# Step one's nucleus search: Newton and secant steps on GpSimd instead of halvings, and no verifying pass on VectorE

## The chip, the cores and the metric

The kernel runs on one core of a Trainium2 chip. The metric is the device time of one execution, in microseconds. The core's engines run side by side and meet only through semaphores: TensorE (PE, with its weight loads as PEld), VectorE (DVE), ScalarE (ACT), GpSimd (POOL) and SyncE (SP), which here issues all DMAs.

## The reference, cut to what matters

```python
h = relu(layernorm(x)); x = x + A @ (h @ W + b) / deg        # x is 3327 x 256, adj 3327 x 3327
X = relu(layernorm(x))
for s in range(2):                                            # STEPS
    A = adj_from_feats(Xa, W1, W2, W3)
    Xf, Xb, Xa = Rf @ Xf, Rb @ Xb, A @ Xa
    Z = Z + Xf @ U1[s] + Xb @ U2[s] + Xa @ U3[s]
# out = x + layernorm(X + Z) * gamma + beta

def adj_from_feats(Xa, W1, W2, W3):
    logits = (Xa @ W1) @ W2 @ (Xa @ W3).T
    # each row: sort, softmax, keep the largest entries until their sum reaches P_NUC = 0.9,
    # the rest to -inf, softmax again
```

So for each of the 3327 rows a cut has to be found in 3327 exponentials: the smallest set of the largest entries that holds 0.9 of the row's sum. The kernel doesn't sort; it searches a threshold.

## The kernel before, in words

Rows go in T = 26 tiles of 128. Three blocks follow one another: the transposed adjacency and the first layer; a short middle block; and `diffusion_step(s)` for s = 0 and 1 ("step zero" and "step one"), which is where the change lies. In a step the engines run the same sweep over i from -2 to 27, each its own instruction stream in the written order; in one body, i is the tile whose sums with the adjacency run on PE (L1398), j = i+1 the tile in the second half of its search, m = i+2 the tile whose logits come in, k = i-1 the tile whose masked exponentials are multiplied with xa. The exponentials of a tile live in one of three buffers `pb`.

In step one the path of a tile is: PE makes its logits in four chunks (L1317). VectorE takes them out of PSUM (`take_logits`, L1206) and reduces the negated row maximum (`negmax`, L1211). ScalarE exponentiates with a row sum (L878). Then the search: in each of 3 + 3 levels ScalarE makes two sums at the present threshold t, the sum of relu and the sum of sign (L896 and L901, `sums`). The first three levels (SUB = ROUGH[1] = 3) look at 832 of the columns (WSUB), the other three at all 3327. GpSimd turns the sums of a level into the mass above t, compares it with the target and moves t up or down by a fixed factor (`level`, L797 to L825); it then lets ScalarE go on (L823) or, after the last level, VectorE (L825). Most instructions there are linked: each waits for the one before.

VectorE (`search`, from L1009) waits for `p_ready`, picks the tightest bracket from the points tried (`bracket`), interpolates a threshold in it (`towards`), makes a verifying pass over all columns at it (L1061), puts the result into the bracket (L1063 to L1066), interpolates again, and makes the cut pass (L1070), which keeps what lies below the cut. It takes the eight largest of each of 16 segments (L1075), then the first chunks of logits of tile m; sorts the candidates in five rounds of eight (L1080, L1082), taking the other logits after the second round; a prefix sum (L1093) finds the exact boundary; 16 MATCH_REPLACE8 take the kept values out (L1134), and the mask pass L1137 subtracts the rest from `pb`. PE then transposes (L1344), ScalarE copies to `pt` (L920), PE multiplies with `xa` (L1352). If the boundary does not lie among the sorted values, `settle` (L1227 on) does more rounds over the whole tile.

What sets the order: ScalarE's body is pt 0, pt 1, z copy, sums of j's level three, pt 2, pt 3, sums of j's level four, xo, exponential of m, sums of m's level zero, the two sums of j's level five with the copies to zt between, sums of m's level one, t_hi and t256, sums of m's level two, t_hi and t256 again. GpSimd's body is `spread` of k (L781), `add_z` (L787), the identity added to `at` (L838), levels three and four of j, the goal and level zero of m, level five of j, levels one and two of m. Tile 0 of step one has only the three subset levels on ScalarE; VectorE makes its three full ones as passes (L1023).

Of the kernel before, what the change touches and what calls it, by code (L numbers as in the profile page):

```python
# [44 lines left out]
def gnn_program(nc, x, adj, W, b, W1, W2, W3, U1, U2, U3, gamma, beta, out):  # L45
# [29 lines left out]
    AIM = (6.0, 16.0)  # L75
    CUT_AIM = (6.0, 24.0)
    VERIFIED = (0, 1)
# [3 lines left out]
    MARGIN = 0.45  # L81
    MOVES = []
    for rough, fine in zip(ROUGH, BISECTIONS):
        half = RANGE / 2 ** (rough + 1) + (MARGIN if rough else 0.0)
        MOVES.append([RANGE / 2 ** (e + 2) for e in range(rough)] + [half / 2 ** (e + 1) for e in range(fine)])
    GMAX, RMAX = max(SEGMENTS), max(SORTED)
    KMAX = 2 + max(b + v for b, v in zip(BISECTIONS, VERIFIED)) + 1
# [3 lines left out]
    FIRST_BISECTIONS = (1, 0)  # L91
# [23 lines left out]
    def sb(name, shape, dt):  # L115
        return nc.alloc_sbuf_tensor(name, shape, dt)
# [35 lines left out]
    padone = sb("padone", [P, 1], f32)  # L152
    early = below[:, :]
# [54 lines left out]
    lower, upper = ends[:, 0:4:2], ends[:, 1:4:2]  # L208
    cur = sb("cur", [P, 2], f32)
    is_lower = sb("is_lower", [P, 1], i32)  # L210
    is_upper = sb("is_upper", [P, 1], i32)
# [13 lines left out]
    over = [sb(f"over{u}", [P, 8], f32) for u in range(3)]  # L225
# [105 lines left out]
    with nc.Block() as block:  # L331
# [39 lines left out]
        def _(pool):  # L371
            nc.gpsimd.memset(ident[:, :], 0.0).then_inc(sem("const_chain"), 1)
            nc.gpsimd.memset(padone[:, :], 1.0).then_inc(sem("const_chain"), 1)
            for u in range(2):
                nc.gpsimd.memset(adj_in[u][:, N:NP], 0.0).then_inc(sem("adj_pad"), 1)
# [297 lines left out]
    def diffusion_step(s):  # L673
# [4 lines left out]
        def S(name):  # L678
            return sem(f"step_{name}")
# [23 lines left out]
        with nc.Block() as block:  # L703
# [67 lines left out]
            def _(pool):  # L771
# [17 lines left out]
                def goal(j):  # L789

                    u = j.third
                    pool.wait_ge(S("exp"), j.n + 1)
                    share = nucleus_pad[:, :] if j.t == T - 1 else NUCLEUS
                    nc.gpsimd.tensor_scalar(targets[u][:, :], mass[u][:, 0:1], share, None, ALU.mult)
                    ch.link(nc.gpsimd.tensor_scalar(over[u][:, 5:6], mass[u][:, 0:1], (NUCLEUS - 1.0) * WSUB / N, None, ALU.mult))

                def level(j, e):  # L797
# [4 lines left out]
                    if e == 0:  # L802
                        goal(j)
                    o, g = over[u], f + 1
                    t = rough_t[u][:, e:e + 1] if f < 0 else thr[u][:, 2 + f:3 + f]
                    up, down = math.exp(MOVES[s][e]), math.exp(-MOVES[s][e])
                    pool.wait_ge(S3("sums")[u], levels_before(s, j.t) + e + 1)
                    ch.link(nc.gpsimd.tensor_scalar(o[:, 2:3], o[:, 1:2], float(WSUB if f < 0 else N), t, ALU.add, ALU.mult))  # L808
                    if f < 0:
                        m, enough = o[:, 3:4], o[:, 5:6]  # L810
                        ch.link(nc.gpsimd.tensor_scalar(m, o[:, 2:3], -0.5, o[:, 0:1], ALU.mult, ALU.add))  # L811
                    else:
                        m, enough = mass[u][:, 2 + f:3 + f], targets[u][:, :]
                        ch.link(nc.gpsimd.tensor_scalar(m, o[:, 2:3], 0.5, o[:, 0:1], ALU.mult, ALU.add))
                    if g < BISECTIONS[s]:
                        ch.link(nc.gpsimd.tensor_scalar(o[:, 4:5], m, enough, up - down, ALU.is_ge, ALU.mult))  # L816
                        if g < 0:
                            ch.link(nc.gpsimd.tensor_scalar(rough_t[u][:, e + 1:e + 2], o[:, 4:5], down, t, ALU.add, ALU.mult))  # L818
                        else:
                            ch.link(nc.gpsimd.tensor_scalar(thr[u][:, 2 + g:3 + g], o[:, 4:5], down, t, ALU.add, ALU.mult))  # L820
                            if not last:
                                ch.link(nc.gpsimd.tensor_scalar(minus_t[u][:, g:g + 1], thr[u][:, 2 + g:3 + g], -1.0, None, ALU.mult))
# [4 lines left out]
                pool.wait_ge(S("search_consts"), 1)  # L827
                ch = Chain(pool, f"step_levels_{s}")
# [37 lines left out]
            def _(act):  # L866
# [13 lines left out]
                def sums(j, n):  # L880
# [6 lines left out]
                    t, sign = (rough_t[u][:, e:e + 1], -1.0) if e < SUB else (minus_t[u][:, e - SUB:e - SUB + 1], 1.0)  # L887
                    before = levels_before(s, j.t)
# [103 lines left out]
            def _(dve):  # L992
# [16 lines left out]
                def search(i):  # L1009
# [8 lines left out]
                    for e in range(AB, BISECTIONS[s]):  # L1018
# [6 lines left out]
                        if e < BISECTIONS[s] - 1:  # L1025
                            d = MOVES[s][SUB + e]
# [413 lines left out]
```

## Time and profile before

| | us |
|---|---|
| median of 3 runs | 2397.59 (2395.61 to 2397.72) |
| the profiled execution, its span | 2397.4 (no other time of it is given) |
| PE busy | 1968.8 (82%) |
| VectorE busy | 1946.8 (81%) |
| ScalarE busy | 1708.7 (71%) |
| GpSimd busy | 873.0 (36%) |
| mean granted TensorE clock | 0.932 |

Rows of the trace give a start and a length in us, the engine, the line, the operation, out<-in, and in brackets how long the engine was idle before and who ended the idle time. "POOLq" or "DVEq" is an engine's sequencer, which issues the semaphore increments that stand alone. Times of instructions are from one profiled execution.

### The profile page before, as it was taken

The page shows a single profiled execution, that of the slowest core. Times are in us where ns is not written, and L with a number is a line of the kernel's source. Part 1 is how long each engine was busy: PE and PEld are TensorE (multiplying, and loading weights), DVE is VectorE, ACT ScalarE, POOL GpSimd, SP SyncE. Part 2 cuts the span into 40 slices and gives each one's busy share as a digit, 9 for nine tenths or more (in the row PEclk, how much of TensorE's full clock was granted, in tenths as well). Part 3 has the DMA queues.
Part 4 walks back from the last instruction along what each step waited for, and adds up shares of the span by engine and source line. Part 5 has one row for each costly group of instructions (what it writes and reads, how often), then busy time and mean ns, then how long its engine had stood idle before and what let it go on. Part 6 is the DMA issues. An engine that isn't in the chain of part 4 may idle for free. (4 is left out here: it accounts for less than half of the span.)

```text
span 2397.4 us, 33017 instructions
## 1 busy us (share of the span) xinstructions
PE 1968.8 (82%) x10002; PEld 1296.6 (54%) x10002; DVE 1946.8 (81%) x6082; ACT 1708.7 (71%) x1806; POOL 873.0 (36%) x1438
## 2 busy tenths in 40 slices
PE   2999753999999999999945979798888888888883
PEld 1555322666666666666623555565655556555552
DVE  6777657788888888888647888988888888898885
ACT  4443236888888888888437888888887888888840
POOL 2000042344444444444433353443435344343423
PEclk9999876999999999999977999999898999999996
DMA  6777221011111111111160001001010100101023
GB/s 229 280 282 289 95 97 36 28 50 50 50 50 48 50 50 46 39 43 50 41 228 18 21 21 40 21 21 41 21 40 21 41 21 21 41 21 40 20 70 125
DMA packets 65726, 167.62 MB, mean 70 GB/s; under 512 B 7037, under 2 KB 45307, under 8 KB 61947
## 3 DMA queue, kind: packets, MB, share of 16 engines
q1 hardware_dynamic: 65530, 165.43, 19.9%
q8 instruction: 72, 1.18, 0.2%
q14 instruction: 124, 1.02, 0.1%
HBM read 117.95 MB, written 47.45 MB: 69 GB/s over the span
## 5 line engine op out<-in xcount | busy, mean ns | idle before, releaser
L1352 PE MATMUL banks<-xa,pt 128*128 128x256 f32 x2704 | 683.3, 407 | 126.0 <-ACT pt L920 125.9
L1352 PEld LDWEIGHTS banks<-xa,pt 128*128 128x128 f32 x2704 | 533.4, 203 | 283.3 <-ACT pt L920 139.6
L896 ACT ACTIVATE junk_a<-pb_all,minus_t 128x3327 f16<-128x3327 f32 x151 | 463.9, 3072 | 150.1 <-POOLq L823 147.5
L901 ACT ACTIVATE junk_a<-pb_all,minus_t 128x3327 f16<-128x3327 f32 x151 | 463.3, 3068 | 2.6
L1398 PE MATMUL banks<-region,at 128*128 128x512 f16 x2028 | 450.4, 381 | 0.0
L808 POOL TENSOR_SCALAR over<-over,points 128x1 f32<-128x1 f32 x151 | 164.7, 1091 | 740.5 <-ACT junk_a L901 740.4
L1398 PEld LDWEIGHTS banks<-region,at 128*128 128x128 f16 x2028 | 199.5, 98 | 231.1 <-issue 6.0
L1206 DVE TENSOR_SCALAR_CACHE_REDUCE pb_all<-banks 128x1024 f32<-128x1024 f32 x260 | 210.9, 849 | 96.6 <-PE banks L1317 93.8
L1317 PE MATMUL banks<-keys,qs 64*128 64x512 f32 (+1 forms) x832 | 199.8, 576 | 90.8 <-DVE pb_all L1206 50.2
L1344 PE MATMUL banks<-ident,pb_all 128*128 128x128 f32 x1352 | 191.7, 291 | 54.5 <-DVE pb_all L1137 34.4
L1075 DVE MAX8 junk_v<-below 128x8 f32<-128x208 f32 (+1 forms) x624 | 222.5, 432 | 2.2
L878 ACT ACTIVATE pb_all<-pb_all,negmax 128x3327 f32<-128x3327 f32 x52 | 159.4, 3065 | 72.4 <-DVE negmax L1211 72.4
L920 ACT ACTIVATE pt<-banks 128x896 f32<-128x896 f32 x208 | 173.0, 861 | 51.1 <-PE banks L1344 50.2
L1344 PEld LDWEIGHTS banks<-ident,pb_all 128*128 128x128 f32 x1352 | 168.6, 151 | 68.6 <-issue 56.8
L1070 DVE SCALAR_TENSOR_TENSOR below<-pb_all,cur 128x3327 f32<-128x3327 f32 x52 | 203.8, 3920 | 1.9
L1317 PEld LDWEIGHTS banks<-keys,qs 64*128 64x128 f32 x832 | 69.8, 193 | 176.6 <-DVE pb_all L1206 71.0
L1023 DVE SCALAR_TENSOR_TENSOR below<-pb_all,points 128x3327 f32<-128x3327 f32 x31 | 114.2, 3685 | 51.9 <-POOLq L825 51.8
L533 PE MATMUL banks<-region,at 128*128 128x512 f16 x676 | 151.5, 381 | 0.0
L1406 PE MATMUL banks<-u_sb,zt 128*128 128x256 f32 x624 | 148.5, 388 | 1.1 <-ACT zt L956 1.1
L1134 DVE MATCH_REPLACE8 below<-junk_v,below 128x208 f32<-128x208 f32 x416 | 143.6, 359 | 0.0
L896 ACT ACTIVATE junk_a<-pb_all,rough_t 128x832 f16<-128x832 f32 x78 | 77.1, 989 | 75.1 <-POOLq L823 72.0
L1406 PEld LDWEIGHTS banks<-u_sb,zt 128*128 128x128 f32 x624 | 114.3, 190 | 16.7 <-ACT zt L953 1.5
(222 smaller groups left out, 2914.1 us busy)
## 6 DMA issues: line engine op xcount, KB each, us to landing
at<-adjT_d SPq DMA_DIRECT2D x52, 832.0 KB, 4.9
region<-in_adj_dram SPq DMA_DIRECT2D x25, 1663.5 KB, 7.9
adjT_d<-at SPq DMA_DIRECT2D x26, 832.0 KB, 3.9
fb_d<-fb_sb SPq DMA_DIRECT2D x26, 256.0 KB, 2.0
region<-fb_d SPq DMA_DIRECT2D x2, 3328.0 KB, 18.1
y_d<-y_sb SPq DMA_DIRECT2D x50, 128.0 KB, 1.9
x_d<-pb_all SPq DMA_DIRECT2D x1, 3328.0 KB, 10.4
qs<-q_d SPq DMA_DIRECT2D x104, 32.0 KB, 4.2
```

The costliest lines, as they stand in the source:

```text
L808: ch.link(nc.gpsimd.tensor_scalar(o[:, 2:3], o[:, 1:2], float(WSUB if f < 0 else N), t, ALU.add, ALU.mult))
L896: nc.scalar.activation(junk_a[:, 0:w], pb[u][:, 0:w], ACT.Relu, scale=sign, bias=t, accum_out=over[u][:, 0:1])\
L901: nc.scalar.activation(junk_a[:, 0:w], pb[u][:, 0:w], ACT.Sign, scale=sign, bias=t, accum_out=over[u][:, 1:2])\
L920: nc.scalar.activation(pt[sl][:, 0:n * P], pt_ps[sl][:, 0:n * P], ACT.Copy).then_inc(S2("pt")[sl], 1)
L1070: ch.link(nc.vector.scalar_tensor_tensor(out=below[:, 0:N], in0=p, scalar=cut, in1=p, op0=ALU.is_lt, op1=ALU.mult, accum_out=below_sum[:, :]))
L1075: ch.add(nc.vector.max(cand[:, 8 * g:8 * g + 8], below[:, g * W8:(g + 1) * W8]))
L1206: nc.vector.tensor_scalar(halves_of_p[:, h:h + n, a:a + w], halves_of_bank[:, h:h + n, 0:w], 1.0, -3.0e38, ALU.mult, ALU.max, accum_out=mi ...
L1317: nc.tensor.matmul(pt_ps[c % 2][:, h * CW:h * CW + w], qs[j.slot][r, :], keys[r, s * HW + c0:s * HW + c0 + w], start=True, stop=True).then ...
L1344: last = nc.tensor.transpose(pt_ps[sl][:, t * P:(t + 1) * P], p[:, (t0 + t) * P:(t0 + t + 1) * P], ident[:, :])
L1352: last = nc.tensor.matmul(bank[4][:, 0:D], pt[sl][:, t * P:(t + 1) * P], xa[:, t0 + t, :], start=(t0 + t == 0), stop=(t0 + t == T - 1))
L1398: last = nc.tensor.matmul(bank[5 + n][:, :], at[i.slot][:, t, :], mov, start=(t == 0), stop=(t == T - 1))
L1406: last = nc.tensor.matmul(bank[7][:, 0:D], zt[:, q, :], u_sb[:, q // KD, q % KD, :], start=(q == 0), stop=(q == 5))
```

## The change

In step one a level no longer moves the threshold by a fixed factor. From the two sums GpSimd gets the count and the sum of the entries below t. On the three subset levels it makes a Newton step for the sum below to equal the wanted tenth; on the first full level a Newton step that aims beyond the target by OVERSHOOT thresholds to one side or the other; on the second full level a secant step from the last two points, with an aim of 12; the third full level only notes its mass. Each step has a division, made as a power of -1 (`ALU.pow` with `minus_one`, a new constant). ScalarE reads the threshold with a sign of -1, so the negated copy `minus_t` goes in step one. The goal has an instruction more. VectorE's verifying pass, its comparisons and its second interpolation go; the cut's aim is 20 instead of 24 thresholds. Tile 0 of step one has a fourth level on ScalarE and GpSimd, and VectorE makes its other two full levels as passes, with a secant step between them. Step zero keeps its halvings; its goal has one instruction less.

```diff
-    AIM = (6.0, 16.0)
-    CUT_AIM = (6.0, 24.0)
-    VERIFIED = (0, 1)
+    CUT_AIM = (6.0, 20.0)
+    OVERSHOOT = 20.0
+    SECANT_AIM = 12.0
...
-    FIRST_BISECTIONS = (1, 0)
+    FIRST_BISECTIONS = (1, 1)
...
+                    ch.link(nc.gpsimd.tensor_scalar(targets[u][:, :], mass[u][:, 0:1], share, None, ALU.mult))
+                    ch.link(nc.gpsimd.tensor_tensor(over[u][:, 8:9], mass[u][:, 0:1], targets[u][:, :], ALU.subtract))
+                    ch.link(nc.gpsimd.tensor_scalar(over[u][:, 5:6], over[u][:, 8:9], WSUB / N, None, ALU.mult))
+
+                def newton(j, e):
...
+                    ch.link(nc.gpsimd.tensor_scalar(count, o[:, 1:2], float(WSUB if f < 0 else N), 0.5, ALU.add, ALU.mult))
+                    ch.link(nc.gpsimd.tensor_scalar(low, count, t, gap, ALU.mult, ALU.subtract))
+                    if f >= 0:
+                        ch.link(nc.gpsimd.tensor_scalar(mass[u][:, 2 + f:3 + f], low, -1.0, mass[u][:, 0:1], ALU.mult, ALU.add))
+                    if f < 1:
+                        ch.add(nc.gpsimd.tensor_scalar(count, count, low, 1e-20, ALU.mult, ALU.max))
+                        if f < 0:
+                            ch.link(nc.gpsimd.tensor_scalar(b, low, wanted, gap, ALU.subtract, ALU.mult))
+                        else:
+                            ch.add(nc.gpsimd.tensor_scalar(a, low, wanted, 2.0 * OVERSHOOT, ALU.is_ge, ALU.mult))
+                            ch.link(nc.gpsimd.tensor_scalar(b, low, wanted, 2.0, ALU.subtract, ALU.mult))
+                            ch.link(nc.gpsimd.tensor_scalar(a, a, OVERSHOOT, t, ALU.subtract, ALU.mult))
+                            ch.link(nc.gpsimd.tensor_scalar(b, b, a, gap, ALU.add, ALU.mult))
+                        ch.link(nc.gpsimd.tensor_tensor(count, count, minus_one[:, :], ALU.pow))
+                        ch.link(nc.gpsimd.tensor_scalar(b, b, count, t, ALU.mult, ALU.subtract))
+                        if f < 0:
+                            ch.link(nc.gpsimd.tensor_scalar(to, b, -1.0, 0.5, ALU.mult, ALU.min))
+                        else:
+                            ch.link(nc.gpsimd.tensor_scalar(b, b, -1.0, 1.0, ALU.mult, ALU.min))
+                            ch.link(nc.gpsimd.tensor_scalar(to, b, 1e-5, None, ALU.max))
+                    elif f == 1:
+                        ch.add(nc.gpsimd.tensor_scalar(b, t, SECANT_AIM, low, ALU.mult, ALU.subtract))
+                        ch.add(nc.gpsimd.tensor_tensor(a, t, thr[u][:, 2:3], ALU.subtract))
+                        ch.link(nc.gpsimd.tensor_tensor(low, low, o[:, 6:7], ALU.subtract))
+                        ch.add(nc.gpsimd.tensor_scalar(count, low, low, 1e-16, ALU.mult, ALU.max))
+                        ch.link(nc.gpsimd.tensor_scalar(b, b, wanted, a, ALU.add, ALU.mult))
+                        ch.link(nc.gpsimd.tensor_tensor(count, count, minus_one[:, :], ALU.pow))
+                        ch.link(nc.gpsimd.tensor_scalar(b, b, low, count, ALU.mult, ALU.mult))
+                        ch.link(nc.gpsimd.tensor_scalar(b, b, t, 1.0, ALU.add, ALU.min))
+                        ch.link(nc.gpsimd.tensor_scalar(to, b, 1e-5, None, ALU.max))
...
+                    if not first and e >= SUB:
+                        t, sign = thr[u][:, 2 + e - SUB:3 + e - SUB], -1.0
...
-                    for v in range(VERIFIED[s]):
-                        towards(cur[:, 0:1], AIM[s])
-                        ch.link(nc.vector.scalar_tensor_tensor(out=below[:, 0:N], in0=p, scalar=cur[:, 0:1], in1=p,
-                                                               op0=ALU.is_ge, op1=ALU.mult, accum_out=cur[:, 1:2]))
-                        nc.vector.tensor_scalar(is_lower[:, :], cur[:, 1:2], tg, None, ALU.is_ge)
-                        ch.link(nc.vector.tensor_scalar(is_upper[:, :], cur[:, 1:2], tg, None, ALU.is_lt), hold=True)
-                        nc.vector.copy_predicated(lower, is_lower[:, :].to_broadcast([P, 2]), cur[:, :])
-                        ch.link(nc.vector.copy_predicated(upper, is_upper[:, :].to_broadcast([P, 2]), cur[:, :]))
                     towards(cur[:, 0:1], CUT_AIM[s])
```

On a subset level f is below 0; f = 0, 1, 2 are the three full levels. In `newton`, as before, two increments follow the instructions: `point`, for which ScalarE's next sums wait, and after the last level `p_ready`, for which VectorE waits.

## Rows read from the trace of the kernel before

**Rows 1.** Busy time by engine in a stretch, step one's steady part; columns as headed.

```profile
core 0: us, PE busy (x) PEld busy (x) DVE busy (x) ACT busy (x) POOL busy (x), PEclk, DMA share, GB/s
1323.48:2249.11 925.63, 794.55 (x3742) 524.33 (x3740) 811.75 (x3080) 759.69 (x837) 386.54 (x682) 0.93 0.09 28
```

**Rows 2.** Chain of waits through step one: start us, us, what.

```profile
1323.48 2.95 issue
...
1659.32 2.95 issue
...
1680.75 6.24 PE banks L1352 x14
...
1702.15 2.95 issue
...
1723.58 4.98 PE banks L1352 x14
...
1743.89 2.95 issue
...
2249.11 2.95 issue
```

**Rows 3.** VectorE's waits, 1323.48 to 2249.11: us in total, times, longest us.

```profile
DVE pb_all L1206 <- PE banks L1317: 67.0, 44, 3.0
```

**Rows 4.** Timeline of three engines in one turn: start us, us, engine, line.

```profile
1755.61 3.62 DVE L1137 TENSOR_TENSOR pb_all<-pb_all,below 128x3327 f32<-128x3327 f32 x1
...
1756.41 2.95 POOL L808 TENSOR_SCALAR over<-over,points 128x1 f32<-128x1 f32 x1 [5.53 <-ACT junk_a L901]
...
1759.46 0.27 POOL L814 TENSOR_SCALAR points<-over 128x1 f32<-128x1 f32 x1
...
1760.01 0.29 POOL L808 TENSOR_SCALAR over<-over,rough_t 128x1 f32<-128x1 f32 x1 [0.29 <-POOL points L814]
...
1760.40 0.27 POOL L811 TENSOR_SCALAR over<-over 128x1 f32<-128x1 f32 x1
...
1760.77 0.29 POOL L816 TENSOR_SCALAR over<-over 128x1 f32<-128x1 f32 x1
...
1761.15 0.31 POOL L818 TENSOR_SCALAR rough_t<-over,rough_t 128x1 f32<-128x1 f32 x1
...
1761.55 0.99 ACT L896 ACTIVATE junk_a<-pb_all,rough_t 128x832 f16<-128x832 f32 x1 [2.22 <-POOLq L823]
...
1762.11 3.68 DVE L1061 SCALAR_TENSOR_TENSOR below<-pb_all,cur 128x3327 f32<-128x3327 f32 x1
...
1763.84 2.09 POOL L808 TENSOR_SCALAR over<-over,rough_t 128x1 f32<-128x1 f32 x1 [2.38 <-ACT junk_a L901]
```

**Rows 5.** GpSimd's groups by line, whole run: busy us, mean ns, idle before.

```profile
L822 POOL TENSOR_SCALAR minus_t<-points 128x1 f32<-128x1 f32 x125 | 27.9, 223 | 10.9
...
L620 POOL TENSOR_SCALAR region<-xa 128x256 f16<-128x256 f32 x26 | 25.4, 978 | 27.1 <-ACT xa L638 25.1
```

**Rows 6.** Timeline where step one begins, around 1294 to 1303.

```profile
1294.30 3.69 DVE L1061 SCALAR_TENSOR_TENSOR below<-pb_all,cur 128x3327 f32<-128x3327 f32 x1
1294.32 3.74 POOL L816 TENSOR_SCALAR over<-over 128x1 f32<-128x1 f32 x1
...
1298.50 0.99 ACT L896 ACTIVATE junk_a<-pb_all,rough_t 128x832 f16<-128x832 f32 x1 [4.30 <-POOLq L823]
...
1302.28 1.22 PE L1352 MATMUL banks<-xa,pt 128*128 128x256 f32 x2 [10.10 <-ACT pt L920]
```

**Rows 7.** Busy time and granted clock in the first product's beginning, columns as rows 1.

```profile
1680.70:1683.90 3.20, 3.15 (x8) 2.52 (x9) 2.95 (x15) 2.10 (x3) 2.57 (x7) 0.50 0.00 0
```

**Rows 8.** ScalarE's timeline in the head of step one.

```profile
1237.01 0.99 ACT L901 ACTIVATE junk_a<-pb_all,rough_t 128x832 f16<-128x832 f32 x1
...
1264.86 3.07 ACT L896 ACTIVATE junk_a<-pb_all,minus_t 128x3327 f16<-128x3327 f32 x1 [3.59 <-POOLq L823]
```

**Rows 9.** Timeline near the end of step one, tile 25's full levels.

```profile
2287.66 0.44 PE L1385 MATMUL banks<-ident,xo_sb 128*128 128x128 f32 x2 [1.92 <-ACT xo_sb L938]
...
2289.70 3.07 ACT L896 ACTIVATE junk_a<-pb_all,minus_t 128x3327 f16<-128x3327 f32 x1 [2.10 <-POOLq L823]
```

More of the change, by code:

```diff
@@ L80, in gnn_program @@
     WSUB = (N + 1) // 4
[L81 to L85, printed above, removed]
+    MOVES = [RANGE / 2 ** (e + 2) for e in range(BISECTIONS[0])]
     GMAX, RMAX = max(SEGMENTS), max(SORTED)
-    KMAX = 2 + max(b + v for b, v in zip(BISECTIONS, VERIFIED)) + 1
+    KMAX = 2 + max(BISECTIONS) + 1
     MOST = max(ACT_BISECTIONS)
-    FIRST_BISECTIONS = (1, 0)
+    FIRST_BISECTIONS = (1, 1)
     LEVELS = [[r + f] + [r + a] * (T - 1) for r, f, a in zip(ROUGH, FIRST_BISECTIONS, ACT_BISECTIONS)]
@@ L152, in gnn_program @@
     padone = sb("padone", [P, 1], f32)
+    minus_one = sb("minus_one", [P, 1], f32)
     early = below[:, :]
@@ L207, in gnn_program @@
     lows, highs = ends[:, 1:3], ends[:, 0:4:3]
[L208 to L211, printed above, removed]
+    cur = sb("cur", [P, 1], f32)
     frac = sb("frac", [P, 4], f32)
@@ L224, in gnn_program @@
     minus_t = [sb(f"minus_t{u}", [P, MOST], f32) for u in range(3)]
-    over = [sb(f"over{u}", [P, 8], f32) for u in range(3)]
+    over = [sb(f"over{u}", [P, 12], f32) for u in range(3)]
     unsettled = sb("unsettled", [P, 1], f32)
@@ L793, in goal @@
                     share = nucleus_pad[:, :] if j.t == T - 1 else NUCLEUS
-                    nc.gpsimd.tensor_scalar(targets[u][:, :], mass[u][:, 0:1], share, None, ALU.mult)
-                    ch.link(nc.gpsimd.tensor_scalar(over[u][:, 5:6], mass[u][:, 0:1], (NUCLEUS - 1.0) * WSUB / N, None, ALU.mult))
+                    if first:
+                        nc.gpsimd.tensor_scalar(targets[u][:, :], mass[u][:, 0:1], share, None, ALU.mult)
+                        return
+                    ch.link(nc.gpsimd.tensor_scalar(targets[u][:, :], mass[u][:, 0:1], share, None, ALU.mult))
@@ new lines, in goal @@
+                    ch.link(nc.gpsimd.tensor_tensor(over[u][:, 8:9], mass[u][:, 0:1], targets[u][:, :], ALU.subtract))
+                    ch.link(nc.gpsimd.tensor_scalar(over[u][:, 5:6], over[u][:, 8:9], WSUB / N, None, ALU.mult))
+                def newton(j, e):
+                    u, last, f = j.third, e == LEVELS[s][j.t] - 1, e - SUB
+                    o = over[u]
+                    t = rough_t[u][:, e:e + 1] if f < 0 else thr[u][:, 2 + f:3 + f]
+                    to = rough_t[u][:, e + 1:e + 2] if f < -1 else thr[u][:, 3 + f:4 + f]
+                    count, gap = o[:, 2:3], o[:, 0:1]
+                    low = o[:, 6 + f:7 + f] if f in (0, 1) else o[:, 3:4]
+                    wanted = o[:, 5:6] if f < 0 else o[:, 8:9]
+                    a, b = o[:, 9:10], o[:, 10:11]
+                    ch.link(nc.gpsimd.tensor_scalar(count, o[:, 1:2], float(WSUB if f < 0 else N), 0.5, ALU.add, ALU.mult))
[28 more added lines that the diff above has]
+                        ch.link(nc.gpsimd.tensor_scalar(to, b, 1e-5, None, ALU.max))
+                    pool.sem_inc(S3("point")[u], 1)
+                    if last:
+                        pool.sem_inc(S("p_ready"), 1)
@@ L803, in level @@
                         goal(j)
+                    pool.wait_ge(S3("sums")[u], levels_before(s, j.t) + e + 1)
+                    if not first:
+                        newton(j, e)
+                        return
                     o, g = over[u], f + 1
-                    t = rough_t[u][:, e:e + 1] if f < 0 else thr[u][:, 2 + f:3 + f]
-                    up, down = math.exp(MOVES[s][e]), math.exp(-MOVES[s][e])
-                    pool.wait_ge(S3("sums")[u], levels_before(s, j.t) + e + 1)
@@ L808, in level @@
[L808 to L814, printed above, removed]
+                    t = thr[u][:, 2 + f:3 + f]
@@ L815, in level @@
+                    up, down = math.exp(MOVES[e]), math.exp(-MOVES[e])
+                    ch.link(nc.gpsimd.tensor_scalar(o[:, 2:3], o[:, 1:2], float(N), t, ALU.add, ALU.mult))
+                    m, enough = mass[u][:, 2 + f:3 + f], targets[u][:, :]
+                    ch.link(nc.gpsimd.tensor_scalar(m, o[:, 2:3], 0.5, o[:, 0:1], ALU.mult, ALU.add))
                     if g < BISECTIONS[s]:
                         ch.link(nc.gpsimd.tensor_scalar(o[:, 4:5], m, enough, up - down, ALU.is_ge, ALU.mult))
[L817 to L822, printed above, removed]
+                        ch.link(nc.gpsimd.tensor_scalar(thr[u][:, 2 + g:3 + g], o[:, 4:5], down, t, ALU.add, ALU.mult))
+                        if not last:
+                            ch.link(nc.gpsimd.tensor_scalar(minus_t[u][:, g:g + 1], thr[u][:, 2 + g:3 + g], -1.0, None, ALU.mult))
```

18 lines of the change are left out of this document (16 added, 2 removed).

## The prediction

> **What bounds the kernel now.** I read, in this order, the busy shares of step one's steady stretch, the chain of waits through it, who waits for whom, and one tile's timeline. In the stretch no engine is full: of 925.6 us PE is busy 794.6, VectorE 811.8, ScalarE 759.7, GpSimd 386.5 [rows 1]. So it is a loop of latencies, and the reader should look for what repeats. The chain [rows 2] repeats once a tile at each exponential: 42.83 us for one tile, 41.74 for the next; from 1323.48 to 2249.11 there are 22 turns, 42.07 on average. A turn, seen from the exponential at 1743.89, is: exponential and two short sums on ScalarE; two full sums; GpSimd's last level of tile j (L808, L814); GpSimd's level one of tile m; ScalarE's two subset sums, the t_hi copies and the first pt copy; then PE's products and logits; VectorE's last take of logits; next exponential. VectorE is on this loop after the logits only: from there to the mask pass (L1137) the diff changes nothing. Before the logits it waits for PE, 67.0 us in 44 waits, about 3 a tile [rows 3]. The verifying pass lies there, in VectorE's slack.
>
> What VectorE does to GpSimd matters more. L808, ready at 1756.41, takes 2.95 us and ends when the mask pass, 1755.61 + 3.62, does; L808 at 1763.84 takes 2.09 and ends just behind the verifying pass, 1762.11 + 3.68. Undisturbed neighbours take 0.27 to 0.31 [rows 4]. A VectorE pass over two SBUF operands holds back any GpSimd instruction that follows it, to its end. By SBUF — State Buffer in the Trainium skill, section "Who interferes with whom", a DVE instruction with two SBUF inputs contends with a GpSimd instruction that reads SBUF, and the second fully blocks; the trace agrees (2.95 and 2.09 against 0.3). Were the port shared by bandwidth instead, the same change would give the second rival below.
>
> **What goes.** Per tile: the pass of 3.68 [rows 4] and about a dozen small VectorE instructions, some 5.5 us. VectorE then waits for PE that much longer: gain on the loop 0, since the last logits and all behind them come when PE brings them. The cut pass (L1070) moves up into the very place of the verifying pass, as soon as the bracket and one `towards` are done, so the port is not free there either; only the second meeting, with `spread`, goes, and that is off the loop. minus_t goes on two levels, ScalarE's sums cost the same.
>
> **What comes, on GpSimd.** A linked instruction steps to the next in 0.37 (two constants, L811), 0.38 (one pointer, L816) or 0.41 (L808); an unlinked one costs about its duration, 0.29 [rows 4]. A subset level becomes 7 instructions, one unlinked, for 4. Their starts, from the level's first: 0, 0.37, 0.78, 1.07, 1.48 (the power), 1.78 + X, 2.19 + X (the one that writes the threshold). X is what the power costs beyond an ordinary small instruction of 0.2. No row shows a power; the bounds are the smallest instruction, 0.22, and the longest elementwise one, 128x256, 0.98 [rows 5], so X is 0 to 0.75. I take 0.3, nearer the small end as the width is one column. Levels three and four grow from 5 to 12 instructions, about 1.8 to 4.4 + X; the last from 2 to 3, +0.4; the goal from 2 to 3.
>
> **The step that decides.** Today level one of tile m starts at 1760.01 and lets ScalarE go at 1761.55; VectorE's pass starts at 1762.11: it misses the pass by 0.6 [rows 4]. Both start from the last level of tile j and shift by the same 0.41. Then the level's first instruction starts at 1760.42, its last one at 1762.61 + X, and the pass at 1762.52, or 0.03 to 0.3 later if the instruction before holds the port. The last instruction therefore falls behind the pass for every X above -0.09, and ScalarE goes on at about 1766.45 + X, 1766.75, not 1761.55: +5.2. The trace already has this case once: at 1294.30 the pass starts, at 1294.32 L816 is caught for 3.74, ScalarE idles 4.30, and PE idles 10.10 [rows 6].
>
> Next, the PE: its first product (L1352 x14) takes 4.98 in one turn and 6.24 in another [rows 2]. Where the turn has the 6.24, it lasts 42.83 instead of 41.74. After a longer idle I expect the 6.24 each time: in its first 3.2 us the granted clock was 0.50, the 1.2 GHz level, after an idle of some 4 us [rows 7], and the product behind the idle of 10.10 took about as long. So a turn is 42.83 + 5.2 = 48.0, or +6.0 on the average of 42.07.
>
> What hides the rest. Level two of tile m now starts behind the pass: unblocked it takes 2.46 + X and frees ScalarE's next full sum some 4.4 late, under the 5.2. Level three comes in front of the third full sum, and adds 2.6 + X to ScalarE's side; ScalarE is through at 45.6 of the turn, PE and VectorE bring the next maximum at 48.0: hidden, with 2 us of cover; a power of X = 2 would use it up. Level four (4.2 + X) lies beside the exponential and two short sums, 5.5 us: hidden. Level zero and the goal lie beside a full sum of 3.07: hidden. The subset levels' unblocked `spread` and `add_z` are far from any reader.
>
> **Head and tail of the step.** Tile 0 has a fourth level on ScalarE and two VectorE passes less. Today the third subset sum of tile 0 ends at 1238 and tile 1's first full sum starts at 1264.86 [rows 8]. After: two levels in front +2.7, level two 2.8, two full sums 6.4 (2 x 3.07 and readout), so about 1250; level three, 4.7; then VectorE's three passes with gaps of 1.6 and 2.3, from 1255 to 1270. Tile 1's three subset levels meet these passes and its full sum starts about 1278: +13. Its next full level adds 2.9 in front of the exponential of tile 2. Mask pass and last level no longer meet there, but level one's block is as long as today's. Head: +17. At the end tiles 24 and 25 have no exponential in front; the last subset threshold comes 4.4 late, then PE waits for xo and ScalarE for level four ([rows 9]: 1.92 and 2.10 today). Level three adds 2.9, and the last tile's VectorE chain, 5.5 shorter, gives back up to where PE's flags hold it, some 3.7: together -0.8.
>
> **Sum.** The profiled execution's span is 2397.4 (no other time of it is shown), 0.2 under the median of 2397.59. 2397.4 + 17 (head) + 22 x 6.0 = 132 + 4.4 - 0.8 = 2550.0; with the 0.2, 2550. Step zero: only its goal loses one instruction, in front of a wait: 0.
>
> **Rivals.**
> 1. *Costly power.* X = 2 rather than 0.3 (a row of 0.98 for 128x256 speaks against it, the missing row for it). ScalarE then ends later than PE: a turn of about 51.3, 22 x 9.2 = 203, head 25: 2630. At X = 0.75, still as forecast, about 2565; at X = 0, 2542.
> 2. *The level slips in front of the pass*, or the port is shared. Then only instructions count: a turn is +1.4 (0.41 and three more instructions, 1.0), and level two is caught in place of it, off PE's path: 22 x 1.4 = 31, head 15: 2443. For it: the miss is 0.09 + X only. Against: X must be negative, and a sharing port would not show 2.95 and 3.74.
> 3. *Not slower.* VectorE's relief reaches the loop through the port: level two is no longer held 1.78 a tile (2.09 less 0.31), ScalarE's full sum starts earlier and sets pt for PE. At most 22 x 1.78 = 39: 2358. This decides only if the level's three added instructions and the third of the last level together cost less than the 0.56 us by which level one now misses the pass; four instructions at 0.29 at least are 1.16 [rows 4]. Two places of the loop would have to be wrong.
> 4. *The search ends worse*: without the checked bracket a row's boundary may fall outside the 40 sorted values, and extra rounds run (L1227 on, never entered in the trace). Three full passes at 3.7 and four rounds of a maximum and a replacement over 3335 columns are some 40 us a tile. For it: 128 rows of 26 tiles must all hit. Against: three threshold points by secant lie close, and the cut aims 20 elements deep in 40. One to three tiles: 2590 to 2670.
>
> **Chances and range.** Forecast 0.73, costly power 0.09, slipping 0.10, worse search 0.04, not slower 0.04. The forecast's own range is 2530 to 2580. The range to hold 8 in 10 reaches into both neighbours, 2480 to 2620. Of the 0.04, half is faster by over 0.2%: 0.02; within 0.2%, about what a measurement of this kernel can tell from no change, 0.02; slower 0.96.
>
> **What would show it.** Turn of the chain near 48; GpSimd's last instruction of level one 3 to 4 us long and behind L1070; ScalarE's wait in front of L896 on the subset from 2.22 to about 7; PE's idle before L1352 near 9 to 10 a tile; first product near 6.2 each time; VectorE's wait before the first logits up by 5. Wrong if no threshold instruction of level one is over 0.5 us (then 2), if the power's own spacing is above 1 (then 1), if the turn stays under 42 (then 3), or if L1228 appears (then 4).

## The result, and the profile after

| | before | after |
|---|---|---|
| median of the runs taken together | 2397.65 us (2395.61 to 2399.72) | 2548.39 us (2547.39 to 2550.83) |
| profiled execution, span | 2397.4 us | 2545.9 us |
| ratio | | 1.0627, 95% interval 1.0612 to 1.0642 |

The forecast was 2550, its range 2480 to 2620. The page of the kernel after begins with busy time by engine (us, share of the span, instructions):

```profile
PE 1968.0 (77%) x10002; PEld 1292.3 (51%) x10002; DVE 1787.6 (70%) x5721; ACT 1713.1 (67%) x1810; POOL 1045.4 (41%) x2035
```

The steady part of step one, from tile 3's exponential to tile 25's, columns as in [rows 1]:

```profile
core 0: us, PE busy (x) PEld busy (x) DVE busy (x) ACT busy (x) POOL busy (x), PEclk, DMA share, GB/s
1339.97:2391.18 1051.21, 793.15 (x3742) 521.36 (x3741) 677.11 (x2772) 757.97 (x837) 543.08 (x1212) 0.89 0.08 25
```

PE and ScalarE do what they did, VectorE has 135 us less to do, GpSimd 157 more, and the stretch is 1051.21 us instead of 925.63: 22 turns of 47.78 instead of 42.07. That is 125.6 of the 148.5 us between the two spans. The head (exponential of tile 0 to that of tile 3) went from 98.4 to 116.1, +17.7; the tail from 148.3 to 154.7, +6.4; what lies before, -1.2.

One turn of the chain of waits in the kernel after (start us, us, what), for [rows 2]:

```profile
1769.77 2.95 issue
...
1782.27 2.92 POOL over L806
...
1788.49 3.89 POOL over L820
...
1792.75 1.09 ACT junk_a L938 x2
...
1796.53 5.87 PE banks L1398 x14
...
1817.55 2.95 issue
```

L806 is the first instruction of tile j's last level, held by the mask pass as L808 was before. L820 is new on the chain: it is an instruction of 0.4 us that takes 3.9. The timeline of that place shows why, for [rows 4]:

```profile
1781.51 3.62 DVE L1183 TENSOR_TENSOR pb_all<-pb_all,below 128x3327 f32<-128x3327 f32 x1
...
1782.27 2.91 POOL L806 TENSOR_SCALAR over<-over 128x1 f32<-128x1 f32 x1 [4.03 <-ACT junk_a L943]
...
1786.30 0.19 POOL L806 TENSOR_SCALAR over<-over 128x1 f32<-128x1 f32 x1 [0.28 <-POOL points L809]
...
1787.82 0.56 POOL L819 TENSOR_TENSOR over<-over,minus_one 128x1 f32<-128x1 f32 x1
...
1788.42 3.69 DVE L1116 SCALAR_TENSOR_TENSOR below<-pb_all,cur 128x3327 f32<-128x3327 f32 x1
1788.49 3.88 POOL L820 TENSOR_SCALAR over<-over,rough_t 128x1 f32<-128x1 f32 x1
...
1792.45 0.22 POOL L822 TENSOR_SCALAR rough_t<-over 128x1 f32<-128x1 f32 x1
...
1792.75 0.99 ACT L938 ACTIVATE junk_a<-pb_all,rough_t 128x832 f16<-128x832 f32 x1 [7.55 <-POOLq L836]
```

Level one of tile m begins at 1786.30. VectorE's cut pass (L1116) starts 2.12 later, 0.07 ahead of L820, which then ends 0.26 behind the end of the pass. L820 and L822, the two instructions behind the power, are thus through only after the pass, and ScalarE's subset sum, idle for 2.22 before [rows 4], is idle for 7.55. VectorE and PE wait for it in turn (who waits for whom, 1350 to 2380: us in total, times, longest):

```profile
DVE pb_all L1252 <- PE banks L1363: 309.9, 63, 11.0
...
ACT junk_a L938 <- POOLq L836: 211.0, 65, 7.9
PE banks L1398 <- ACT pt L962: 210.6, 22, 9.6
```

VectorE's wait for logits was 67.0 us [rows 3] and is 309.9, or 11.0 a turn more: the 6.1 a turn that VectorE has less to do are spent in that wait, and some 5 more. The power by itself, among GpSimd's groups by line (busy us, mean ns, idle before), beside an ordinary instruction of two inputs:

```profile
L819 POOL TENSOR_TENSOR over<-over,minus_one 128x1 f32<-128x1 f32 x104 | 58.8, 566 | 8.7
...
L828 POOL TENSOR_TENSOR over<-points 128x1 f32<-128x1 f32 x25 | 4.8, 193 | 2.0
```

### The profile page after: what moved, and what is told of

It reads as the page before. It is cut to its first block, busy times and chain, and to the rows that moved or that the text cites. A ratio compares the mean times of both kernels' runs of the same rounds, so it can differ in the third digit from the quotient of the medians.

```text
span 2545.9 us, 33233 instructions
## 1 busy us (share of the span) xinstructions
PE 1968.0 (77%) x10002; PEld 1292.3 (51%) x10002; DVE 1787.6 (70%) x5721; ACT 1713.1 (67%) x1810; POOL 1045.4 (41%) x2035
## 4 chain that ended last, share of the span: by engine, by line
PE 17%; POOL 11%; ACT 11%; issue 10%; DVE 3%; DMA 0%; POOLq 0%; ACTq 0%; DVEq 0%; SPq 0%
PE banks L1398 13%; ACT junk_a L943 5%; POOL over L820 4%; ACT junk_a L938 3%; PE banks L1363 3%; POOL over L806 3%; DVE pb_all L1252 2%; PE banks L1390 1%; POOL over L807 1%; POOL over L819 1%; ACT pt L962 1%; POOL over L813 1%; DVE region L1326 1%; DVE region L1321 0%; ACT zt L995 0%
## 5 line engine op out<-in xcount | busy, mean ns | idle before, releaser
L1398 PE MATMUL banks<-xa,pt 128*128 128x256 f32 x2704 | 694.4, 412 | 271.1 <-ACT pt L962 271.1
L1398 PEld LDWEIGHTS banks<-xa,pt 128*128 128x128 f32 x2704 | 541.8, 207 | 431.0 <-ACT pt L962 283.4
L938 ACT ACTIVATE junk_a<-pb_all,minus_t 128x3327 f16<-128x3327 f32 x76 | 233.5, 3073 | 106.4 <-POOLq L862 106.1
L806 POOL TENSOR_SCALAR over<-over 128x1 f32<-128x1 f32 x154 | 95.6, 621 | 479.9 <-ACT junk_a L943 473.3
L938 ACT ACTIVATE junk_a<-pb_all,points 128x3327 f16<-128x3327 f32 x76 | 233.4, 3071 | 69.5 <-POOLq L836 67.2
L854 POOL TENSOR_SCALAR over<-over,points 128x1 f32<-128x1 f32 x76 | 85.7, 1127 | 423.8 <-ACT junk_a L943 423.8
L943 ACT ACTIVATE junk_a<-pb_all,points 128x3327 f16<-128x3327 f32 x76 | 233.3, 3070 | 1.7
L943 ACT ACTIVATE junk_a<-pb_all,minus_t 128x3327 f16<-128x3327 f32 x76 | 233.0, 3066 | 0.9
L962 ACT ACTIVATE pt<-banks 128x896 f32<-128x896 f32 x208 | 172.9, 860 | 79.5 <-PE banks L1390 79.5
L1390 PE MATMUL banks<-ident,pb_all 128*128 128x128 f32 x1352 | 178.2, 277 | 52.8 <-DVE pb_all L1183 34.1
L1116 DVE SCALAR_TENSOR_TENSOR below<-pb_all,cur 128x3327 f32<-128x3327 f32 x52 | 192.1, 3694 | 1.9
L1390 PEld LDWEIGHTS banks<-ident,pb_all 128*128 128x128 f32 x1352 | 156.0, 143 | 66.1 <-issue 54.8
```

Of the source, the lines that this page charges most:

```text
L806: ch.link(nc.gpsimd.tensor_scalar(count, o[:, 1:2], float(WSUB if f < 0 else N), 0.5, ALU.add, ALU.mult))
L938: nc.scalar.activation(junk_a[:, 0:w], pb[u][:, 0:w], ACT.Relu, scale=sign, bias=t, accum_out=over[u][:, 0:1])\
L943: nc.scalar.activation(junk_a[:, 0:w], pb[u][:, 0:w], ACT.Sign, scale=sign, bias=t, accum_out=over[u][:, 1:2])\
L962: nc.scalar.activation(pt[sl][:, 0:n * P], pt_ps[sl][:, 0:n * P], ACT.Copy).then_inc(S2("pt")[sl], 1)
L1390: last = nc.tensor.transpose(pt_ps[sl][:, t * P:(t + 1) * P], p[:, (t0 + t) * P:(t0 + t + 1) * P], ident[:, :])
L1398: last = nc.tensor.matmul(bank[4][:, 0:D], pt[sl][:, t * P:(t + 1) * P], xa[:, t0 + t, :], start=(t0 + t == 0), stop=(t0 + t == T - 1))
```

## The experiments

The theory (the port): a long VectorE pass over two SBUF operands holds the next small GpSimd instruction to its end, so that the two engines meet not only through semaphores; the loop loses 5 us a turn because the last instructions of the longer level one no longer start before the pass does. Its rivals: the time is the sum of the instructions added; or it is the power; or it is the verifying pass's own doing.

**e1 and e2: how many small instructions until the step.** The kernel before, with idle instructions put into level one of tile m; two in e1, three in e2.

```diff
+                        for _ in range(2 if e == 1 else 0):      # e2: 3
+                            ch.link(nc.gpsimd.tensor_scalar(o[:, 7:8], o[:, 2:3], -0.5, o[:, 0:1], ALU.mult, ALU.add))
```

> The kernel before, with two more linked GpSimd instructions of one column in level one only (they write an unused column). Port theory (a VectorE pass over two SBUF operands holds the level's last instruction if that starts behind the pass): the last instruction starts at 1761.15 + 0.75 = 1761.90, still before the pass at 1762.11, so only the instructions count: a turn is +0.8, 22 turns +18, the granted clock up to 15 more: 2415 to 2435. Rival (what a level costs is the sum of its instructions, wherever the pass lies): the same, 2415.

> As the last one with three such instructions instead of two, 0.37 us more. Port theory: the last instruction would start at 1762.28, behind the pass at 1762.11, and is held to its end at 1765.8; ScalarE goes on 4.5 us later than in the kernel before, and the first product on PE takes the longer form: +5 a turn, 2500 to 2520. Rival (sum of instructions): 22 x 1.1 = 24, 2422 to 2445.

Measured: 2412.01 (ratio 1.0051, 1.0034 to 1.0067) with two, 2520.52 (1.0508, 1.0490 to 1.0525) with three; before 2399.63. Both lie outside what I had written, 3 us under the range and 0.5 over it. From e1 to e2, one instruction of 0.37 us a turn costs 108.5 us; the rival's 22 x 0.37 is 8. The turn goes from 42.64 to 47.20 on average, 4.6 more, which is 100 of it; head and tail have the rest. The first two instructions together cost 0.6 a turn. GpSimd's last instruction of the level and VectorE's verifying pass, first in e1, then in e2:

```profile
1683.93 0.26 POOL L820 TENSOR_SCALAR rough_t<-over,rough_t 128x1 f32<-128x1 f32 x1
...
1684.17 3.68 DVE L1063 SCALAR_TENSOR_TENSOR below<-pb_all,cur 128x3327 f32<-128x3327 f32 x1
```

```profile
1673.27 3.69 DVE L1063 SCALAR_TENSOR_TENSOR below<-pb_all,cur 128x3327 f32<-128x3327 f32 x1
...
1673.42 3.67 POOL L820 TENSOR_SCALAR rough_t<-over,rough_t 128x1 f32<-128x1 f32 x1
```

0.24 ahead of the pass it takes 0.26; 0.15 behind its start it takes 3.67. What counts is when the last instruction starts: in e1 it ends at 1684.19, when the pass has begun, and is not held. This is a staircase, with no Newton step, no power and no pass removed.

**e3: keep the Newton steps, and take the collision away.** The kernel after; VectorE starts the cut pass of tile i when level one of tile i + 1 has ended.

```diff
+                    if not first and (i + 1).inside(T):
+                        dve.wait_ge(S3("point")[(i + 1).third], levels_before(s, (i + 1).t) + 2)
                     ch.link(nc.vector.scalar_tensor_tensor(out=below[:, 0:N], in0=p, scalar=cut, in1=p, ...
```

> The changed kernel, and VectorE waits with the cut pass of tile i until GpSimd has finished level one of tile i+1; all work stays. Port theory: the level's two last instructions are no longer held, ScalarE goes on 3.5 us earlier in each turn, a turn of 44.2 for 47.8: 2469 (2455 to 2485), though a wait was only added. Rival (sum of instructions): no change, 2548. Rival (VectorE's own time bounds the turn): slower than 2548, as the cut pass comes later.

Measured: 2468.88 (1.0289, 1.0272 to 1.0306). In its timeline L820 is short again, and the pass pays 0.96 for it:

```profile
1669.87 0.39 POOL L820 TENSOR_SCALAR over<-over,rough_t 128x1 f32<-128x1 f32 x1
1670.35 0.22 POOL L822 TENSOR_SCALAR rough_t<-over 128x1 f32<-128x1 f32 x1
1670.72 3.68 DVE L1118 SCALAR_TENSOR_TENSOR below<-pb_all,cur 128x3327 f32<-128x3327 f32 x1 [0.96 <-POOLq L836]
```

The turn is 44.39 on average. So of the change's 5.71 a turn, 3.39 are the collision and 2.32 the instructions themselves, with whatever VectorE's wait costs. A wait added to VectorE saves 79.5 us.

**e6: the same pass, with one SBUF operand.** The kernel after; the cut pass is replaced by an instruction that reads only p. It does not cut, and the flag for further rounds is held at zero.

```diff
-  ch.link(nc.vector.scalar_tensor_tensor(out=below[:, 0:N], in0=p, scalar=cut, in1=p, op0=ALU.is_lt, op1=ALU.mult, accum_out=below_sum))
+  ch.link(nc.vector.tensor_scalar(below[:, 0:N], p, 1.0, -3.0e38, ALU.mult, ALU.max, accum_out=below_sum))
```

> The changed kernel with step one's cut pass made by an instruction that reads one SBUF operand (times 1, maximum, with accumulator) and so doesn't cut; the flag for extra rounds is held at zero. The pass is as long. Port theory: with one SBUF operand it doesn't hold GpSimd, level one's last two instructions run through, a turn of about 44.2: 2469 (2450 to 2485). Rival (any long VectorE instruction that writes SBUF slows GpSimd): no change, 2548.

Measured: 2463.75 (1.0269, 1.0252 to 1.0286), a turn of 44.39 like that of e3. L820 starts inside the pass and is not held:

```profile
1709.54 3.62 DVE L1120 TENSOR_SCALAR_CACHE_REDUCE below<-pb_all 128x3327 f32<-128x3327 f32 x1
1709.61 0.39 POOL L820 TENSOR_SCALAR over<-over,rough_t 128x1 f32<-128x1 f32 x1
```

Of the passes seen here, those with two SBUF operands hold GpSimd and this one does not. The Trainium skill says in SBUF — State Buffer, "Who interferes with whom", that a VectorE instruction with two SBUF inputs contends with a GpSimd instruction that reads SBUF, and that one with at most one SBUF input, outside the modes that use both ports, does not. This run agrees with it: same place, same width, one operand fewer, no hold (0.39 against 3.88).

**e7: the power replaced by an addition.** The kernel after; its thresholds are then not the search's, and the flag is held at zero.

```diff
-  ch.link(nc.gpsimd.tensor_tensor(count, count, minus_one[:, :], ALU.pow))
+  ch.link(nc.gpsimd.tensor_tensor(count, count, minus_one[:, :], ALU.add))
```

> The changed kernel with each power on GpSimd replaced by an addition, so the thresholds are not those of the search; the flag for extra rounds is held at zero. It measures the power's own price: 0.37 us (0.56 against 0.19). Port theory: the instruction behind the power now starts 0.3 before the pass, but the last one still behind it: a turn is shorter only by what comes behind the pass, 0.3: with the head 2538 (2530 to 2545). Rival (the powers' cost adds up, five a turn): 22 x 1.9 = 41 less, 2507.

Measured: 2533.39 (1.0559, 1.0542 to 1.0577). The instruction falls from 566 to 190 ns, the kernel by 15.0 us, the turn from 47.78 to 47.44. The held instruction is now the last one, L822, as the prediction had it for the kernel after:

```profile
1780.11 3.69 DVE L1116 SCALAR_TENSOR_TENSOR below<-pb_all,cur 128x3327 f32<-128x3327 f32 x1
1780.26 3.61 POOL L822 TENSOR_SCALAR rough_t<-over 128x1 f32<-128x1 f32 x1
```

It misses by 0.15, where the prediction's 0.09 + X gives 0.09. So X = 0 is not enough to slip ahead of the pass; where the limit lies no run shows.

**e4: the Newton steps with the verifying pass put back.**

```diff
+                    for v in range(VERIFIED[s]):        # VERIFIED = (0, 1), AIM = (6.0, 16.0)
+                        towards(cur[:, 0:1], AIM[s])
+                        ...
                     towards(cur[:, 0:1], CUT_AIM[s])
```

> The changed kernel with the verifying pass, its comparisons and second interpolation back on VectorE: so the GpSimd part of the change alone. Port theory: the verifying pass stands where the cut pass was and holds level one just as long; the cut pass now holds level two, which frees ScalarE's full sum 2.6 later and makes ScalarE the last to come: a turn of 49.1, 2577 (2560 to 2595). Rival (the work taken from VectorE counts in full): +5.5 a turn, 2670.

Measured: 2617.81 (1.0910, 1.0892 to 1.0928): a miss, 41 us above the theory's value and 23 above its range. The rival, +5.5 a turn, is out: an undisturbed turn is 48.76 (forecast 49.1), 0.98 more than the kernel after's, which gives 22 x 0.98 = 21.6; tile 3's exponential comes 7.3 later. What was not foreseen is in one tile near the end: between the exponentials at 2176.13 and 2360.35 lie three turns and 37.9 us more. The chain of waits there:

```profile
2240.34 3.63 DVE pb_all L1286
2244.00 3.70 DVE below L1287 x2
...
2248.11 3.65 DVE top L1273
...
2252.84 3.62 DVE below L1212
```

These are the further rounds of the search, entered once, for four rounds. The kernel after enters them nowhere; why the pass put back leaves one tile unsettled that was settled without it stays open. Of the 72.1 us between the spans of the two kernels (2618.0 and 2545.9) the other 5 lie behind tile 25's exponential. So in the changed kernel, unlike in the old one (e5), the verifying pass would not be free: it would cost about 1 us a turn.

**e5: the halvings without the verifying pass.** The kernel before, with the flag for further rounds held at zero.

```diff
-    VERIFIED = (0, 1)
+    VERIFIED = (0, 0)
-    ... tensor_tensor(unsettled[:, :], none[:, :], flaw[:, :], ALU.max)
+    ... tensor_tensor(unsettled[:, :], none[:, :], none[:, :], ALU.subtract)
```

> The kernel before without the verifying pass, comparisons and second interpolation, and with the flag for extra rounds held at zero in step one, so that rows whose boundary lies outside the sorted values get no extra rounds: the VectorE part of the change alone. Port theory: VectorE only waits longer for the logits and the cut pass stands in the verifying pass's place: turn 42.1 as before, head a few us shorter: 2392 (2385 to 2399). Rival (VectorE's relief counts in full): 22 x 5.5 = 121 less, 2277.

Measured: 2391.10 (0.9969, 0.9959 to 0.9979). Some 3.68 us and a dozen small instructions a tile less on VectorE bring 8.0 us in the kernel. Its turns are 41.73 and 42.75, as before's, and 42.04 on average: the gain is outside them. The forecast "gain on the loop 0" holds; the rival, full relief at 2277, is out.

**e9: the same, with the further rounds kept.** e5's first edit alone.

```diff
-    VERIFIED = (0, 1)
+    VERIFIED = (0, 0)
```

> The kernel before without the verifying pass, and with the further rounds of the search kept. If the halvings leave all rows of all 26 tiles settled without that pass, the time is that of the run in which these rounds were shut off, 2391 (2385 to 2399). If the pass is what keeps rows settled (my rival of a worse search, taken over to the old search), each tile that enters the further rounds costs about 38 us, the price that one such entry had in the run of the new search with the verifying pass put back: 2430 for one, 2470 for two, more for more.

Measured: 96461.66 us, 40.2 times the time of before (40.14 to 40.27). Neither of the two values that I had written came near. VectorE's largest groups:

```profile
L1214 DVE MAX8 top<-below 128x8 f32<-128x3335 f32 x10712 | 38937.1, 3635 | 3140.4 <-issue 3138.0
L1153 DVE MATCH_REPLACE8 below<-take,below 128x3335 f32<-128x3335 f32 x10712 | 38745.9, 3617 | 0.0
```

10712 rounds at 8.78 us each ((96461.7 - 2388.9) / 10712) are the whole difference. The kernel runs the rounds in fixed blocks of 4, 24 and 416; a block that is entered runs whole. In the trace all 26 tiles of step one enter (L1228 x26), two leave after 28 rounds, and 24 run all 444: they had a row that was still open after 28 rounds. How many rounds those rows needed can't be read from it. With these halvings and this aim of the cut (24) the verifying pass can't be left out, and e5 is a measurement of time only: in the old kernel the pass is free in time and keeps the search out of its further rounds. I forecast a price of 38 us an entry from e4, where four rounds were enough; an entry that runs all blocks costs 3.9 ms. Which rows ask for them, and why, stays open, and so does whether another aim would do without the pass.

**e8: Newton steps, with the order built for the port.** The kernel after. ScalarE makes tile m's sums of level one between tile j's last two full sums; GpSimd does level one of m ahead of level five of j; VectorE's mask pass waits for level one of i + 2, and the cut pass for level two of i + 1.

```diff
 GpSimd
+                    if not first:
+                        level(m, 1)
                     level(j, SUB + ACT_BISECTIONS[s] - 1)
 ScalarE
+                    if not first and m.inside(T):
+                        for n in range(2, 4):
+                            sums(m, n)
                     if j.inside(T):
                         for n in STEPS[NT + 1]:
                             sums(j, n)
 VectorE
+                    if not first and (i + 1).inside(T):
+                        dve.wait_ge(S3("point")[(i + 1).third], levels_before(s, (i + 1).t) + 3)
                     ... the cut pass
+                        if (i + 2).inside(T):
+                            dve.wait_ge(S3("point")[(i + 2).third], levels_before(s, (i + 2).t) + 2)
                         ch.add(nc.vector.tensor_tensor(p, p, below[:, 0:N], ALU.subtract))
```

> The changed kernel with the work ordered around the port, all work kept: ScalarE makes m's level-one sums between j's two last full sums, GpSimd does level one of m before level five of j, VectorE waits with the mask pass for level one of tile i+2 and with the cut pass for level two of tile i+1. Port theory: the wait of 2.7 behind the mask pass and that of 3.7 behind the cut pass both go from the loop; a turn of 40.5 against 47.8 and 42.1, head and tail as in the changed kernel: 2390 (2375 to 2410), the first version in which the passes taken from VectorE pay. Rival (sum of instructions): no change from 2548.

Measured: 2382.12 (0.9925, 0.9909 to 0.9942): the fastest of all, 166 us under the kernel after with the same arithmetic, and 17 under the kernel before in the same series (2399.11). The turn settles at 40.96 and is 40.85 on average. Its timeline shows GpSimd's one instruction that is still held, and VectorE's pass waiting:

```profile
1755.30 3.62 DVE L1192 TENSOR_TENSOR pb_all<-pb_all,below 128x3327 f32<-128x3327 f32 x1 [2.65 <-POOLq L836]
```

```profile
1755.00 0.22 POOL L822 TENSOR_SCALAR rough_t<-over 128x1 f32<-128x1 f32 x1
1755.61 3.36 POOL L806 TENSOR_SCALAR over<-over 128x1 f32<-128x1 f32 x1 [0.40 <-ACT junk_a L948]
```

Level one (its last instruction is L822) ends 0.08 before the mask pass starts; the held L806 belongs to level five, for which only VectorE waits.

**e11: that order without VectorE's two waits.**

> The kernel after in the new order, without the two waits of VectorE. If the hold of small GpSimd instructions by VectorE's long passes decides, the order alone gets level one into the way of the mask pass, which without its wait starts about 2.7 us earlier, ahead of the end of level one, and holds one instruction for 3.3 us or so: between 2382 and the 2548 of the kernel after, 2440 (2400 to 2480). If the length of the chain of GpSimd instructions and its place in the order decide, and not the hold, taking the waits away costs nothing: 2382 or less (2365 to 2385).

Measured: 2477.42 (1.0326, 1.0309 to 1.0344), near the upper end of the theory's range. Without the waits level one meets the mask pass, and level two the cut pass (VectorE's rows, then GpSimd's):

```profile
1706.37 3.62 DVE L1188 TENSOR_TENSOR pb_all<-pb_all,below 128x3327 f32<-128x3327 f32 x1
...
1716.06 3.68 DVE L1121 SCALAR_TENSOR_TENSOR below<-pb_all,cur 128x3327 f32<-128x3327 f32 x1
```

```profile
1706.48 3.75 POOL L807 TENSOR_SCALAR over<-over,rough_t 128x1 f32<-128x1 f32 x1
...
1716.28 3.88 POOL L819 TENSOR_TENSOR over<-over,minus_one 128x1 f32<-128x1 f32 x1
```

Each is caught within 0.22 us of the pass's start. The two waits are worth 95.3 us; the order without them is worth 71.0 against the kernel after.

**e10: the same order and waits with the halvings and the verifying pass.** The edits of e8 made to the kernel before, the first wait ahead of the verifying pass.

> The kernel before (halvings and verifying pass) in the order that made the kernel after fast: level one of tile m ahead of level five of tile j on GpSimd, its sums between the last two full sums of j on ScalarE, and VectorE's verifying and mask passes waiting for it. If what made that version fast is the order, which keeps small GpSimd instructions out of VectorE's long passes, it works as well with the shorter halvings: a turn of 40 to 41 in place of 42.07, 2355 (2335 to 2385). If the order repaired only what the Newton steps broke, nothing is gained: 2398 (2390 to 2415).

Measured: 2389.95 (0.9960, 0.9945 to 0.9974), a turn of 41.56 where I had said 40 to 41: between the two theories' ranges, at the edge of the second. The order gains 9.7 us on the kernel before of the same series (2399.64), and half a microsecond a turn. The busy time of one turn and VectorE's waits in it say what is in the way:

```profile
core 0: us, PE busy (x) PEld busy (x) DVE busy (x) ACT busy (x) POOL busy (x), PEclk, DMA share, GB/s
1653.29:1694.85 41.56, 36.50 (x171) 24.18 (x170) 37.16 (x141) 34.46 (x38) 18.07 (x31) 0.92 0.09 30
```

```profile
1666.32 3.62 DVE L1146 TENSOR_TENSOR pb_all<-pb_all,below 128x3327 f32<-128x3327 f32 x1 [1.22 <-POOLq L823]
...
1670.61 0.23 DVE L1042 TENSOR_SCALAR least<-points,target 128x5 f32<-128x5 f32 x1 [0.66 <-POOLq L825]
...
1672.81 0.16 DVE L1051 TENSOR_TENSOR frac<-ends 128x1 f32<-128x1 f32 x1 [1.08 <-POOLq L823]
```

VectorE is busy 37.16 of 41.56 and waits 2.96 for GpSimd; in this turn it waits nowhere for PE's logits. In e8's turns it still does (busy time of one, then a row of the next):

```profile
1699.86:1740.81 40.95, 36.32 (x172) 24.31 (x170) 31.25 (x127) 34.45 (x39) 25.22 (x55) 0.92 0.09 30
```

```profile
1776.38 1.23 DVE L1261 TENSOR_SCALAR_CACHE_REDUCE pb_all<-banks 128x1024 f32<-128x1024 f32 x1 [2.95 <-PE banks L1372]
```

So with level one out of the passes' way VectorE has next to no slack in e10, and the pass that goes is worth something: from e10 to e8, relief less longer levels, 7.8 us, with a turn of 40.85 for 41.56 and a head 12.5 longer. That VectorE bounds e10's turn is inferred from these sums; the chain of waits of that run does not reach back into the turns.

## Why the prediction was right, point by point

The mechanism is the one that was forecast. That 2548.39 lies within 2 us of the 2550 is partly luck: against the sum's span of 2550.0 the turns brought 6.4 less, the head 0.7 more, the tail 2.8 more and what lies before 1.2 less, which makes 2545.9, and the median of the runs lies 2.5 above that profiled span.

- **The step that decides: right.** Level one of tile m fell behind the cut pass, ScalarE went on 5 us late. I had the last instruction caught at X = 0.3; the last two were behind the pass. The cause is the size of X: the power has 566 ns, 0.37 more than the 193 of an ordinary one. So L820 started at 2.19 from the level's first instruction and not at 1.78 + 0.3 = 2.08, and the pass at 2.12 and not at 2.10: 0.07 behind it, not 0.02 ahead. It changes little: from the level's start to ScalarE's next sum it is 6.45 (1786.30 to 1792.75), forecast 6.33. e2 made the same step, 4.6 a turn over e1 and 5.1 over before, without any of the change's arithmetic, e3 and e6 took it away from the changed kernel in two ways (2469, 2464), e7 showed that it stays at X = 0. The "0.6" by which level one misses the pass today is counted from its end; the room is 0.96, from the start of its last instruction (1761.15) to that of the pass (1762.11) [rows 4], as the sum then used it and e1 bears out.
- **The product behind the idle: a size.** The first product took 5.87 us and not 6.24, after an idle of 9.58. Its first 3.2 us show the granted clock of [rows 7] again, but so does the idle before it, and the clock is back at 1754.00 (columns as in [rows 1]):

```profile
1743.80:1748.70 4.90, 0.00 (x0) 0.00 (x0) 4.82 (x19) 3.71 (x8) 2.19 (x6) 0.50 0.00 0
...
1748.74:1751.94 3.20, 3.20 (x8) 2.57 (x9) 0.41 (x3) 2.79 (x3) 2.76 (x6) 0.50 0.00 0
...
1754.00:1754.61 0.61, 0.61 (x5) 0.49 (x4) 0.00 (x0) 0.61 (x1) 0.00 (x0) 1.00 0.00 0
```

  0.50 is the 1.2 GHz level. It holds for the first 5.26 of this product and held for 6.01 of the one of 6.24 in before, so the longer idle does not give the long form each time, as I had it: the term for the product was mis-sized. With the 0.37 less for the product, and 0.12 more for the level, the turn is 47.78 for the 48.0 forecast, and 22 of them bring 125.6 for the 132 of the sum (which rounded 5.93 up to 6.0).
- **Head: right.** +17.7 for 17.
- **Tail: a size.** +6.4 for +3.6. The chain's GpSimd time from tile 25's exponential on is 26.4 us before and 37.2 after: levels three and four of the last tile are both on it (from 1.7 to 4.8 and from 2.3 to 4.5), and I had counted level three alone.
- **What hides the rest: right.** ScalarE waits 1.64 a turn for the next maximum (34.5 us in 21 turns), where I had 2.4 of cover (48.0 less 45.6).
- **VectorE's relief on the loop, 0: right for the kernel before.** e5: turns unchanged, 8.0 us outside them. I had credited some 4 at the end. Behind the longer levels it is not 0: e4 puts the pass back and pays 0.98 a turn. The sum of the forecast did not need this, as it compared the two kernels whole.
- **Before the step:** I put 0, it was -1.2, within what executions of one kernel differ.
- **The rivals.** Costly power: out, 0.57 us. Slipping ahead, or a shared port: out in the kernel as changed. e3 and e6, which make level one run through, give 2469 and 2464, so its sum (2443) was 21 to 26 low: the instructions cost 2.3 a turn where I had 1.4. Not slower: out in the kernel as changed. Worse search: it did not occur (L1273 is never reached), though e9 shows how large the case would have been that I gave 2590 to 2670.

## What to carry to other kernels

Where a short chain of tiny instructions on GpSimd ends just before a long two-operand pass of VectorE, its slack is a number to be read, from the start of the chain's last instruction to the start of the pass. Here it was 0.96 us: two instructions more fitted in and cost 0.6 a turn together, the third, of 0.37, cost 4.6. Before such a chain is lengthened, put it where no such pass can start, by order and by a wait on the engine that has slack; the same Newton steps then took 2382 us and not 2548. And a pass that costs no time may still be what keeps a costly path from being entered: try its removal with that path live.

## What the runs showed of the hardware that I had not expected

- A GpSimd power over one column takes 0.566 us (104 of them), an addition in its place 0.190 (e7).
- A wait can be cheaper than the absence of one: 0.96 us of waiting a turn on VectorE (21.0 in 22 turns) took 79.5 us from the kernel (e3), two waits 95.3 (e11 to e8).
- With TensorE idle through nearly all of e9 (busy 1957.7 of 96461.7 us), its mean granted clock was 0.51 over the run, against 0.93 in the steady part of step one before [rows 1].
